# Query and key biases folded by row sums on VectorE instead of by matmuls, in a gated attention and mixture-of-experts kernel

## The reference, cut to what matters

```python
xn = layernorm(x)                                   # x: 2 batches of 1024 tokens, width 512
q, k, v = split(xn @ w_qkv.T + b_qkv, 3)
s = softmax(q @ k.T / sqrt(512)) @ v @ w_out.T + b_out
h = silu(xn @ expert_w[e] + expert_b[e])            # 8 experts, the two best of a token by router
f = sum of the two h, weighted, @ proj_w + proj_b
g = silu(norm_w * (xn + f) / rms(xn + f))
out = x + s * g
```

## Time and profile before

| | |
|---|---|
| median of 3 runs | 488.39 us (487.38 to 488.58) |
| span of the profiled execution, first to last instruction | 486.1 us |
| PE busy | 474.3 us, 98% of the span |
| DVE, ACT, POOL busy | 317.2, 213.7, 217.8 us |
| granted TensorE clock, mean | 0.998 of full speed |
| moved by DMA | 115.77 MB, 238 GB/s in the mean |

### The profile page before, as it was taken

One profiled execution on the slowest core, in us unless ns is written; L12 is line 12 of the kernel. 1 busy time (PEld: TensorE's weight loads), 2 busy tenths in 40 slices (PEclk: granted clock), 3 DMA queues, 4 the chain that ended last, 5 costly groups with the idle time before them and its releaser, 6 DMA issues.

```text
span 486.1 us, 7132 instructions
## 1 busy us (share of the span) xinstructions
PE 474.3 (98%) x2152; PEld 388.6 (80%) x2153; DVE 317.2 (65%) x472; ACT 213.7 (44%) x310; POOL 217.8 (45%) x317
## 2 busy tenths in 40 slices
PE   6899999999999999999999999999999999999995
PEld 3888786888888888887888888888888878888884
DVE  3966252677653436887988888852597754857762
ACT  2674553143331163744644444423655441644550
POOL 4586110006887849600300000754567873377234
PEclk9999999999999999999999999999999999999999
DMA  8975999947969599978799665987545864445512
GB/s 305 305 237 195 382 374 379 388 162 259 310 256 333 180 330 312 248 223 260 217 260 280 200 201 177 318 282 288 166 162 162 266 191 155 151 137 170 174 42 87
DMA packets 78142, 115.77 MB, mean 238 GB/s; under 512 B 6608, under 2 KB 36320, under 8 KB 78112
## 3 DMA queue, kind: packets, MB, share of 16 engines
q1 hardware_dynamic: 65072, 79.72, 52.1%
q0 software_dynamic: 6896, 23.36, 13.6%
q10 hardware_dynamic: 6144, 12.32, 7.1%
HBM read 66.09 MB, written 49.28 MB: 237 GB/s over the span
## 4 chain that ended last, share of the span: by engine, by line
PE 89%; DVE 5%; DMA 3%; issue 2%; SPq 1%; ACT 0%; DVEq 0%
PE ab L1646 21%; PE ab L1647 20%; PE ab L1648 20%; PE sc L1646 7%; PE sc L1647 7%; PE sc L1648 7%; PE tp L1652 2%; DMA xg<-rows_scratch 2%; DMA raw_v<-in_w_qkv 2%; PE tp L1688 1%; PE sc L1717 1%; DVE stats L1206 1%; PE sc L1720 1%; PE ab L1670 0%; DVE tp L1402 0%
## 5 line engine op out<-in xcount | busy, mean ns | idle before, releaser
L811 POOL DMA_INDIRECT y<-y_scratch,pos x32 | 33.4, 1044 | 78.0 <-DMA y_scratch<-yt_so 63.3
L1646 PE MATMUL ab<-W,st_h 128*128 x156 | 60.8, 390 | 0.7 <-DVE st_l L1343 0.7
L1648 PE MATMUL ab<-W,st_l 128*128 x156 | 60.7, 389 | 0.0
L1647 PE MATMUL ab<-W,st_h 128*128 x156 | 60.7, 389 | 0.0
L794 POOL DMA_INDIRECT rows_scratch<-xb,pos x32 | 31.3, 978 | 50.8 <-DVEq L1331 42.6
L1646 PE MATMUL sc<-xt_h,t_h 128*128 128x512 f32 x128 | 50.1, 391 | 0.0
L1648 PE MATMUL sc<-xt_h,t_l 128*128 128x512 f32 x128 | 49.8, 389 | 0.0
L1647 PE MATMUL sc<-xt_l,t_h 128*128 128x512 f32 x128 | 49.8, 389 | 0.0
L1070 ACT CAST st_h<-tp 128x512 fp32r<-128x512 f32 x39 | 22.9, 587 | 40.4 <-PE ab L1648 38.3
L1410 DVE TENSOR_REDUCE small<-sc 128x1 f32<-128x1024 f32 x16 | 19.5, 1222 | 23.8 <-PE sc L1648 23.6
L1646 PEld LDWEIGHTS ab<-W,st_h 128*128 128x128 f32 x156 | 29.3, 188 | 7.2 <-issue 1.1
(11 more groups left out here) (284 smaller groups left out, 1225.5 us busy)
## 6 DMA issues: line engine op xcount, KB each, us to landing
rows_scratch<-xn ACTq DMA_DIRECT2D x3, 3328.0 KB, 20.1
xb<-in_expert_w POOLq DMA_DIRECT2D x6, 1024.0 KB, 9.8
xn<-rows_scratch SPq DMA_DIRECT2D x48, 128.0 KB, 3.3
xg<-rows_scratch SPq DMA_DIRECT2D x44, 128.0 KB, 3.1
y_scratch<-yt_own SPq DMA_DIRECT2D x20, 256.0 KB, 3.6
y_scratch<-yt_so SPq DMA_DIRECT2D x19, 256.0 KB, 2.9
p_scratch<-prob SPq DMA_DIRECT2D x9, 512.0 KB, 3.2
rows_scratch<-xs SPq DMA_DIRECT2D x16, 256.0 KB, 6.3
```

The source lines that it names most:

```text
L811: pool.indirect_dma_start(y[:, q, :], None, y_d, bass.IndirectOffsetOnAxis(pos[:, GB * s + p:GB * s + p + 1], 0))\
L1646: nc.tensor.matmul(dst, lh, rh, start=start, stop=False)
L1647: nc.tensor.matmul(dst, lh, rl, start=False, stop=False)
L1648: return nc.tensor.matmul(dst, ll, rh, start=False, stop=stop)
```

## The change: what it does

`bias_products`, the copy of `bias_rows` and `turn_biases` go. In their place DVE forms for each weight the sum over its four row blocks, each block weighed by its bias (`weigh_by_biases`: 2 times one scaling and three multiply-adds of 128 x 512), and PE multiplies 128 columns of that sum (every fourth) with a single column of ones: 8 fp32 matmuls with one moving column, which give the columns at once (`bias_columns`). The second fold is made straight after the first, before the turns of 8 and 9, and the third before `bias_columns`. `fold_low` and `fold_high` follow this order. ACT waits for `pre` = 4 (both sums done) before it writes `bt_h`. The third store of zeros is issued by POOL after `batch_stats`, on its own semaphore `zero_last`.

```diff
-            pool.wait_ge(zero_in, 48)
+            pool.wait_ge(zero_in, 32)
+            pool.wait_ge(zero_last, 16)
...
             batch_stats(pool, link, slice(GB, G))
+            pool.wait_ge(zero_set, 1)
+            clear_slots(pool, 2, zero_last)
...
-                if t >= GB - 3:
+                if GB - 3 <= t < GB - 1:
                     act.wait_ge(zero_set, 1)
-                    clear_slots(t - GB + 3)
+                    clear_slots(act, t - GB + 3, zero_in)
...
             fold_high(KC)
-            act.wait_ge(vecs, 2)
-            nc.scalar.copy(bias_rows, ab[0:2, :, :].rearrange("p a n -> p (a n)")).then_inc(rows_out, 1)
+            fold_high(KC + 1)
+            act.wait_ge(pre, 4)
             hi(GB)
             hi(GB + 1)
-            fold_high(KC + 1)
+            fold_high(KC + 2)
...
+            def weigh_by_biases():
+
+                for m, n in ((0, 1), (1, 0)):
+                    dve.wait_ge(qk_in[n], 16)
+                    link(vec.tensor_scalar(weighed[m], raw[n][:, 0, :], bcols[:, m, 0:1], None, ALU.mult))
+                    for c in range(1, KC):
+                        last = vec.scalar_tensor_tensor(weighed[m], raw[n][:, c, :], bcols[:, m, c:c + 1], weighed[m],
+                                                        ALU.mult, ALU.add)
+                        if c < KC - 1:
+                            link(last)
+                    last.then_inc(pre, 1)
...
-                two = lambda m: ab[:, 0, 2 * KC * m:2 * KC * (m + 1)].rearrange("p (c a) -> p c a", a=2)
-                vec.tensor_reduce(tb[:, :], two(0), AX.X, ALU.add).then_inc(pre_done, 1)
+                vec.tensor_copy(tb[:, :], ab[:, 0, 0:KC]).then_inc(pre_done, 1)
...
+            weigh_by_biases()
             fold_low(KC)
+            fold_low(KC + 1)
             lo(GB)
             lo(GB + 1)
-            fold_low(KC + 1)
+            fold_low(KC + 2)
             fold_biases()
...
-            def bias_products():
...
-            def turn_biases():
...
+            def bias_columns():
+
+                pe.wait_ge(pre, 4)
+                for m in range(2):
+                    for n in range(KC):
+                        nc.tensor.matmul(ab[:, 0, KC * m + n:KC * m + n + 1], every_fourth(weighed[m], n), ones[:, 0:1],
+                                         start=True, stop=True)
+                nc.tensor.matmul(ab[:, 0, 2 * KC:3 * KC], ones[:, :], prod, start=True, stop=True).then_inc(vecs, 1)
...
             fold_keys(FOLDS[0])
-            pe.wait_ge(ab_read, 2 + GB)
-            bias_products()
+            fold_keys(FOLDS[1])
             turn(GB)
             turn(GB + 1)
-            fold_keys(FOLDS[1])
-            turn_biases()
+            fold_keys(FOLDS[2])
+            pe.wait_ge(ab_read, 2 + GB)
+            bias_columns()
             turn(GB + 2)
             turn(GB + 3)
-            fold_keys(FOLDS[2])
             fold_keys(FOLDS[3])
```

More of the change, by code:

```diff
@@ L258, in gated_attention_moe @@
                       for v in (pt_h, pt_l))
-        bias_rows = prob[0:2, 0:2 * D]
+        weighed = (prob[:, 0:D], prob[:, D:2 * D])
         lt = (prob[0:2 * NP, :], so[0:2 * NP, :, :].rearrange("p a n -> p (a n)"))
@@ L328, in gated_attention_moe @@
         zero_in = sem("zero_in")
+        zero_last = sem("zero_last")
         send_in = sems("send_in", GB)
@@ L440, in turned, with clear_slots @@
             return (p2_h, p2_l) if j == GB - 2 else (p1_h, p1_l)
+        def clear_slots(eng, n, landed):
+            w = slice(n * SLOT_TILES // 3, (n + 1) * SLOT_TILES // 3)
+            eng.dma_start(rows_t[:, w, :], zeros.to_broadcast([P, w.stop - w.start, D])).then_inc(landed, 16)
         def rsqrt(eng, link, r, v, t):
@@ L924, in t_hi @@
                     .then_inc(ab_hi, 1)
-            def clear_slots(n):
-                w = slice(n * SLOT_TILES // 3, (n + 1) * SLOT_TILES // 3)
-                act.dma_start(rows_t[:, w, :], zeros.to_broadcast([P, w.stop - w.start, D])).then_inc(zero_in, 16)
             for c in range(1, KC):
@@ L975, in _ @@
             hi(GB + 3)
-            fold_high(KC + 2)
             normalise(GB + 6)
@@ L1036, in _ @@
             nc.scalar.activation(small[:, 10, :], small[:, 9, :], ACT.Exp).then_inc(gate_e, 1)
-            act.wait_ge(zero_in, 48)
+            act.wait_ge(zero_in, 32)
+            act.wait_ge(zero_last, 16)
             exp_0(1)
@@ L1255, in fold_biases @@
                 dve.wait_ge(const, 6)
-                dve.wait_ge(vecs, 3)
-                two = lambda m: ab[:, 0, 2 * KC * m:2 * KC * (m + 1)].rearrange("p (c a) -> p c a", a=2)
-                vec.tensor_reduce(tb[:, :], two(0), AX.X, ALU.add).then_inc(pre_done, 1)
-                link(vec.tensor_reduce(rw[:, :, E], two(1), AX.X, ALU.add))
-                vec.tensor_reduce(rb_bc[:, E:E + 1], ab[:, 0, 4 * KC:5 * KC], AX.X, ALU.add).then_inc(pre_done, 1)
+                dve.wait_ge(vecs, 2)
+                vec.tensor_copy(tb[:, :], ab[:, 0, 0:KC]).then_inc(pre_done, 1)
+                link(vec.tensor_copy(rw[:, :, E], ab[:, 0, KC:2 * KC]))
+                vec.tensor_reduce(rb_bc[:, E:E + 1], ab[:, 0, 2 * KC:3 * KC], AX.X, ALU.add).then_inc(pre_done, 1)
                 link(vec.tensor_copy(rw_hl[:, :, 0, :], rw[:, :, :]))
@@ L1371, in _ @@
                 if t == 0:
-                    split_bias()
+                    bias_product()
                 if t == 2:
@@ L1391, in _ @@
             lo(GB + 3)
-            fold_low(KC + 2)
             fold_low(KC + 3)
@@ L1661, in bias_of_values @@
                 pe.wait_ge(fold_l, KC)
-                pe.wait_ge(pre, 3)
+                pe.wait_ge(pre, 2)
                 nc.tensor.matmul(sc[:, 1, 1, :], ones[:, :], bias_sum, start=True, stop=True).then_inc(vecs, 1)
-            def bias_products():
[L1667 to L1674, removed]
-            def turn_biases():
[L1677 to L1681, removed]
+            def bias_columns():
[5 more added lines that the diff above has]
+                nc.tensor.matmul(ab[:, 0, 2 * KC:3 * KC], ones[:, :], prod, start=True, stop=True).then_inc(vecs, 1)
             def turn(g):
```

6 lines of the change are left out of this document (1 added, 5 removed).

## The result

The changed kernel takes 493.8 us in the median of 4 runs (492.3 to 494.7), the kernel before in the same session 488.3 (487.4 to 488.6): a ratio of 1.0101, 95% interval 1.0079 to 1.0123. It is 5.5 us slower, where 1.7 us of gain had been forecast.

What follows compares the result with a forecast made beforehand. PE, busy 474.3 of 486.1 us, was the bound, the row-store chain second. PE's 2.65 us saving, with a new 0.9 us wait for tile 11, gave 1.7 us gained: 484.4 span plus 2.3, 486.7 us (range 485.1 to 488.9).

Steps and rivals of the forecast that it cites:

- two things pull at that ... I let them cancel: Row 9's store landing: hardware queues lose the third zero store, POOL's queue gains it; landing kept at 8.3 us.
- second rival: POOL's zero store as third busy queue delays the stores of rows 8 to 11; 489.8 us, chance 0.13.
- the squeeze: Same as the second rival: three loaded queues slow the row stores, turn 15 starts 1.4 us later; chance 0.13.
- The price of the columns: PE's added one-column fp32 matmuls: 16 pieces at 0.13 us, 2.1 us together (1.1 to 3.7).
- PE's saving: Bias products and transposes removed, 4.73 us, less 2.1 for the columns: 2.65 us less PE work (1.0 to 3.6).
- The delay of POOL: POOL's last three statistics operations slowed beside DVE's multiply-adds, 1.1 us; upper case six operations, 2.3 us, nothing gained.
- the rows' chain: Row 9's store, normalise 13, casts 10 and 11, low parts: tile 11 ready at 65.6, PE waits 0.9 us.
- DVE's sums: Scalings and multiply-adds on idle DVE, 6.0 us from 50.27, ending near 56.3, hidden by 1.4 us before PE comes.
- Nothing behind the changed stage therefore stands ready to eat a gain of 2 or 3 us: After the stage, PE's longest single wait is 0.7 us, at the first experts; so loss was sought inside the stage.
- The fourth rival: The gain is made, then lost at the experts, where transfers end the chain; about 488 us, chance 0.10.

Runs made afterwards that it cites:

- zero_on_act: The change, with the third zero store back in ACT's queue where it was; 490.3 us, ratio 1.0044.
- before_zero_pool: The kernel before, with only its third zero store moved to POOL behind the statistics; 491.7 us, ratio 1.0062.
- mended_but_pool_store: all_mended, but the third zero store is POOL's, behind the statistics, as in the change; 491.2 us, ratio 1.0048.
- plain_columns: zero_late, with the column products' weights read in a row (output not the reference's); 491.5 us, ratio 1.0067.
- mended_but_early_sums: all_mended, but DVE's sums start at once beside POOL's statistics, as in the change; 488.3 us, ratio 0.9993.
- all_mended: The change, with third zero store on ACT behind normalising rows 8 to 11, sums after statistics, weights read in a row; 488.3 us, ratio 0.9992.
- tiles_first: all_mended, with DVE making the low parts of tiles 8 and 9 ahead of the second fold's; 488.7 us, ratio 0.9994.
- zeros_from_36: tiles_first, with the first two zero stores issued earlier, two turns and one turn; 486.1 us, ratio 0.9965.
- zero_late: The change, with POOL's third zero store behind its first two expert loads; 493.0 us, ratio 1.0077.

## Why the prediction was wrong

- **Row 9's store: "two things pull at that ... I let them cancel".** This step failed, and with it the weight of the second rival (0.13). The third queue wins clearly: 8.3 became 12.3 us, and it is back at 8.4 with the zero store on ACT. The rival's price stood: 489.8 forecast for the squeeze against a kernel of 488.4, so 1.4 us of loss where 1.7 of gain had been counted, 3.1 in difference; measured for the zero store's place alone are 3.5 (the change less zero_on_act), 3.5 (before_zero_pool) and 2.9 (mended_but_pool_store), by the ratios 2.8, 3.0 and 2.7. Against the rival stood that POOL writes its descriptors slowly; its issue took 1.24 us. The Trainium skill, page "DMA: Bandwidth & Descriptors", section "Queues, rings and completion order", has the engines go round their queues packet by packet. The trace agrees with that rule: 92, 92 and 90 packets in 2 us, and q0's, with twice the bytes, took half of the engines' time.
- **The price of the columns** was taken as 0.13 us a piece and is 0.22, at the upper bound: 3.5 us instead of 2.1, so PE's saving is 4.73 - 3.53 = 1.2 us and not 2.65. That the stride makes it is shown by plain_columns: with weights in a row 0.106. The nearest row, L1679, has the stride but only two rows of weights; whether that is why it was cheaper, no run shows.
- **The clock** stood in no term. In the profiled execution of the change it falls behind the columns for about 3.5 us. There are 8 matmuls 0.43 apart instead of 0.23, so about 1.6 us; it falls again behind the 2.25 us gap, and the stretch from the first logit row to the turned logits takes 70.1 - 50.9 = 19.2 us instead of 17.7, 1.5 more.
- **The delay of POOL** was taken as three operations, 1.1 us. Six were delayed, from the moment the sums began, and the statistics end 3.3 us later. Of that 0.8 is the later start of this execution: 2.4 us, at the upper end given (2.3), where nothing is gained. Beside a multiply-add they follow each other at 0.79 us, not at the 0.66 of the earlier trace rows. Beside a scaling an operation takes 0.49 us, and a second one 0.32, for 0.20; they end 0.05 and 0.06 us after their scaling. The rule of the Trainium skill on page "SBUF — State Buffer", section "SBUF: two separate sides", by which the scaling blocks POOL too, is borne out by these rows. mended_but_early_sums against all_mended shows the price on the rows' chain, 2.2 us, and that the median is the same.
- **DVE's sums**: right. 5.6 us for 6.0, finished at 56.6, PE comes at 60.3. Reordering folds and turns cost PE at most 0.3 us: the first logit row of plain_columns comes at 46.2, where 47.2, less the saving of 3.0 (4.73 - 1.70), with its pause of 1.7, makes 45.9.
- **"Nothing behind the changed stage therefore stands ready to eat a gain of 2 or 3 us"**: wrong, and read from too narrow a view. PE's waits were short because the transfers landed in time for PE as slow as it was. There is a second bound, DMA engines that are full for over 50 us, and PE's order does not move it; windows with their DMA share show it. It did not decide the change's own loss, but it is the larger part of why tiles_first, 2.5 us ahead at the turned logits, came out at the time of before. In its profiled execution, 1.2 us above its median, the two waits at 111 and 120 and what follows them cost 3.3 us; another 1.0 comes later, in small steps. The fourth rival had the idea (0.10) and the wrong place, the experts.

The sum of the change from first turn to first logit row: 1.2 us less work; 0.6 of waiting and 0.3 of slower turns at tiles 8 and 9; 1.6 for the clock; 2.25 of gap. That is 3.6 of the 3.8 us seen; with the 1.5 behind it 5.3 by the turned logits, close to the 5.5 of the medians (4.9 by the ratio). This sum is read from one trace; shown by runs is the zero store's part of it, 2.7 to 3.5 us. The parts are not independent: the gap would be longer if the clock had not fallen, since tile 11 comes at its own time.

Left open: what exactly lets the clock fall, and in which executions. A profile shows one execution, and the mean clock of the others says that it is not the kernel alone. It lies between 0.995 and 1.000 in 98 executions of the kernel before, but between 0.993 and 1.000 in plain_columns, 0.994 and 0.999 in tiles_first, 0.992 and 1.000 in zeros_from_36, whose profiles show no fall in the stage; and one execution of zero_late, with its strided columns, has 1.000 and takes 493.4 us all the same. What it costs differs too. In zeros_from_36 the eight executions at 0.999 or more took 485.0 to 486.4 us and the four at 0.995 or less 487.0 to 490.0. In tiles_first the six at 0.996 or less took 487.4 to 488.8 and the six above it 488.5 to 490.1, so there the lower clock did not make the kernel slower.

Medians of several sessions of before differ by up to 0.9 us, and the intervals of the ratios reach 0.6 us or more to each side, so that gains smaller than that can't be told.

## What to carry to other kernels

An engine that hardly waits may still have a second bound right behind it: before counting a saving of PE, look how long the DMA share has stood at full where the next transfer is issued that PE waits for. A bulk store beside others that are waited for cost nothing here in a queue that already carried two such stores, and some 3 us in a third queue. It also pushes back what stands behind it: moving two of three such stores 3 to 7 us forward, into a stretch in which the engines were a third busy, turned 0.9994 into 0.9965. A trace shows one execution: look at the clock of the others before calling a fall of it an effect of the kernel. Work put on an idle DVE has to be checked against small chained operations on POOL beside it, and single-column matmuls against the stride of their weights.

## What the runs showed of the hardware that was not expected

- An fp32 weight load of 128 x 128 with one moving column, one of the two passes of such a matmul, took 0.106 us with weights in a row and 0.22 with a stride of four elements.
- In the profiled executions, the granted clock fell to its lower level behind 3.5 us of strided columns wherever they stood, also with turns between two halves. It stayed up behind 1.8 us of plain columns (plain_columns, tiles_first, zeros_from_36), but fell where pauses of 0.17 and 0.63 us joined them (all_mended). It stayed up behind single pauses of 1.70, 1.75, 1.82 and 2.07 us, and fell behind one of 2.25 (the change) and one of 2.32 (mended_but_pool_store). It also fell once in code that all kernels share (zero_late, from 22 us), so none of this is a rule: other executions of the same kernels have other means.
- POOL's operations of 128 x 8 took 0.49 and 0.32 us beside a DVE scaling (0.05 and 0.06 us past its end) and 0.71 beside multiply-adds, 0.20 alone.
- A queue of POOL's, with packets of 4 KB beside two queues with 2 KB, took half of the engines' time.
